# Fetching more single tiles of rows from SyncE and ScalarE in a graph network kernel, with byte offsets kept in the edge records

## What is computed

```python
h = relu(layernorm(x)); x = x + attention(h)      # q[src]·k[dst], softmax over the edges of each dst, sum of v[src]
h = relu(layernorm(x)); x = x + relation(h)       # mean per edge type of (h @ W[type])[other end], edges both ways
h = relu(layernorm(x)); x = x + gine(h)           # sum of h[dst] + attr16 @ We over the edges of each src, then an MLP
h = relu(layernorm(x)); x = x + edge_conv(h)      # relu(sum of (h @ W)[src] + attr6 @ We over the edges of each dst)
```

## Time and profile before

| | us |
|---|---|
| timed, median of 3 runs | 21892.74 |
| timed, lowest and highest | 21871.51, 21898.5 |
| profiled execution, first to last instruction (the span) | 15054.0 |
| median of the timed runs less that span | 6838.7 |

### The profile page before, as it was taken

The page is one execution under the profiler, slowest core; times in us unless marked ns, Lnnn a source line. Parts: engine busy times, 40 slices in busy tenths (PEclk is TensorE's granted clock), DMA queues, the critical chain, the costliest instruction groups (busy, mean ns, idle before and its releaser), DMA issues. The chain is left out here.

```text
span 15054.0 us, 271220 instructions
## 1 busy us (share of the span) xinstructions
PE 8740.4 (58%) x56159; PEld 6734.5 (45%) x56575; DVE 9778.7 (65%) x34050; ACT 2787.6 (19%) x7303; POOL 11087.4 (74%) x11347
## 2 busy tenths in 40 slices
PE   6766667777777777555555555555444444544444
PEld 2212226666666666244444444444333333433334
DVE  8877777777878778866666677777533333433334
ACT  0011114444444444421111111111100000200000
POOL 4777767777777777777777777777677777477776
PEclk8866668999999999865555555555555555655555
DMA  2011122222222222422222222222222222422222
GB/s 85 7 42 50 53 59 74 69 69 69 69 69 69 69 69 67 152 83 59 59 58 59 58 63 63 62 63 63 69 63 63 63 62 60 121 59 59 58 59 68
DMA packets 734382, 992.39 MB, mean 66 GB/s; under 512 B 271737, under 2 KB 534898, under 8 KB 732626
## 3 DMA queue, kind: packets, MB, share of 16 engines
q0 software_dynamic: 387968, 670.55, 17.1%
q1 hardware_dynamic: 324786, 301.13, 6.5%
q10 hardware_dynamic: 20000, 3.33, 0.1%
HBM read 795.25 MB, written 178.86 MB: 65 GB/s over the span
## 5 line engine op out<-in xcount | busy, mean ns | idle before, releaser
L1834 DVE TENSOR_TENSOR acc<-banks,acc 128x128 f32 x3328 | 969.8, 291 | 2616.2 <-PE banks L1792 2247.3
L668 POOL DMA_INDIRECT rec_dst<-stage_dst_sort,row_dst_sort x1563 | 1575.4, 1008 | 641.1 <-issue 474.3
L800 POOL DMA_INDIRECT far_att<-table_qv,recs_att x1664 | 1636.5, 983 | 523.9 <-issue 506.8
L800 POOL DMA_INDIRECT far_sum_dst<-table_h,recs_dst x1613 | 1561.2, 968 | 584.1 <-issue 491.7
L800 POOL DMA_INDIRECT far_sum_src<-table_h,recs_src x1613 | 1572.9, 975 | 558.8 <-issue 491.6
L800 POOL DMA_INDIRECT far_rel_src<-table_xw,recs_rel_src x1638 | 1574.7, 961 | 508.7 <-issue 494.2
L800 POOL DMA_INDIRECT far_rel_dst<-table_xw,recs_rel_dst x1638 | 1561.1, 953 | 510.4 <-issue 494.5
L1622 DVE TENSOR_TENSOR acc<-banks,acc 128x128 f32 x3328 | 969.7, 291 | 1119.2 <-PE banks L1548 1002.5
L936 POOL DMA_INDIRECT rec_src<-moved_att,row_src x1248 | 1245.0, 998 | 397.3 <-issue 379.9
L1792 PE MATMUL banks<-far_sum_src,hot_sum_src 128*128 128x128 f32 x3226 | 825.1, 436 | 1214.9 <-DVE hot_sum_src L1825 831.3
L1792 PE MATMUL banks<-far_sum_dst,hot_sum_dst 128*128 128x128 f32 x3226 | 825.9, 436 | 1147.5 <-DVE hot_sum_dst L1825 899.8
(11 more groups left out here) (343 smaller groups left out, 21302.0 us busy)
## 6 DMA issues: line engine op xcount, KB each, us to landing
lone_sync_rel_dst<-table_xw SPq DMA_DIRECT2D x3328, 0.5 KB
lone_sync_rel_src<-table_xw SPq DMA_DIRECT2D x3328, 0.5 KB
lone_sync_sum_src<-table_h SPq DMA_DIRECT2D x3328, 0.5 KB
lone_sync_sum_dst<-table_h SPq DMA_DIRECT2D x3328, 0.5 KB
lone_scalar_sum_src<-table_h ACTq DMA_DIRECT2D x3200, 0.5 KB
lone_scalar_sum_dst<-table_h ACTq DMA_DIRECT2D x3200, 0.5 KB
table_xw<-xw_rel_tables SPq DMA_DIRECT2D x98, 512.0 KB
far_att<-table_qv,recs_att POOLq DMA_INDIRECT x1664
```

What stands on the lines that cost most here:

```text
L668: e.indirect_dma_start(out=flat_dst, out_offset=bass.IndirectOffsetOnAxis(ap=row["dst"][:, c + i:c + i + 1], axis=0), in_=stage["dst"][:, ...
L800: e.indirect_dma_start(out=self.far[:, g % RING, t, :], out_offset=None, in_=table, in_offset=bass.IndirectOffsetOnAxis(ap=index, axis=0)) ...
L1834: e.tensor_tensor(acc[:, bass.ds(at[t], 1), :], sums[g0 % 4][:, t:t + 1, :], acc[:, bass.ds(at[t], 1), :], ALU.add).then_inc(k.s_sum, 1)
```

## The change

- Each record gets two more words, `OFF` and `OFF8`: where the far row begins in `table_h` and in `table_xw`, in bytes. The dst records get a third, `OFFQ`, for `table_qv`. ACT writes them in `staged`. The column of ones becomes `OFF`; records are 13 and 22 words instead of 11 and 21.
- `single_rows` replaces `number_rows` and `fetch_rows`: it loads 32 registers with one instruction (`LOAD`), and addresses the table as a flat array of bytes at the register's value.
- Single tiles come at a step of their own in each pass (`Lone(buffer, ids, column, tile, first, step)`): SP every 6th group in the attention (69 tiles, which was 0), every 10th in the relation and sum passes (41 tiles each, which was 26); ACT every 16th in the relation passes (25 tiles, which was 0), every 10th in the sum passes (41, which was 25).
- ACT issues its rows a few after each group, in the relation passes behind its copy of that group (L1538), in the sum passes in a loop over the groups.
- In the attention DVE's two operations on gathered rows are split in two in the groups with a single tile.

```diff
-IDX, IDX8, LOC, TYP, ONE, ATT = range(6)
-CD = ATT + 6
+IDX, IDX8, LOC, TYP, OFF, OFF8, ATT = range(7)
+ROW = F * 4
+LOAD = 32
+OFFQ = ATT + 6
+CD = OFFQ + 1
...
         def staged(e, s, j):
+            e.activation(to[:, b, 0:n, OFF].bitcast(I32), node[FAR[s]][:, c:c + n], ACT.Copy, scale=float(ROW))
+            e.activation(to[:, b, 0:n, OFF8].bitcast(I32), idx8[s][:, c:c + n], ACT.Copy, scale=float(ROW))
+            if s == "dst":
+                e.activation(to[:, b, 0:n, OFFQ].bitcast(I32), node[FAR[s]][:, c:c + n], ACT.Copy, scale=float(2 * ROW))
             e.wait_ge(s_att[s][b], 16 * (j // 2 + 1))
...
+class Lone:
+    def __init__(self, buffer, ids, column, tile, first, step):
+        self.buffer, self.ids, self.column, self.tile, self.step = buffer, ids, column, tile, step
+        self.groups = list(range(first, GROUPS, step))
...
-        for p in range(first, first + n, 8):
-            row = e.bass.values_load_multi_w_load_instructions(
-                self.ids[name][0:1, s % 2, p:p + 8], engines=[e.engine], min_val=0, max_val=table.shape[0] - 1,
-            for i in range(8):
-                e.dma_start(self.lone[name][p + i:p + i + 1, s % 2, :], table[bass.ds(row[i], 1), :]).then_inc(self.k.s_lone[name][s % 2], 16)
+    def single_rows(self, e, name, g, n, table, freed):
+        one = self.lone[name]
+        r, end = (min(P * h // one.step, P * len(one.groups)) for h in (g, g + n))
+        width = table.shape[1] * 4
+        flat = table.rearrange("n f -> (n f)").bitcast(U8)
+        while r < end:
+            s, first = divmod(r, P)
+            m = min(P - first, end - r)
+            if first == 0:
+                if s == 0:
+                    self.number_rows(e, name, 0)
+                if s >= 2:
+                    e.wait_ge(*freed(one.groups[s - 2]))
+                e.wait_ge(self.k.s_ids[name], self.ids_base[name] + 16 * (s + 1))
+                if s + 1 < len(one.groups):
+                    self.number_rows(e, name, s + 1)
+            for p in range(first, first + m):
+                if p % LOAD == 0:
+                    one.at = e.bass.values_load_multi_w_load_instructions(
+                        one.ids[0:1, s % 2, p:p + LOAD], engines=[e.engine], min_val=0, max_val=(table.shape[0] - 1) * width,
+                row = flat[bass.ds(one.at[p % LOAD], width)].rearrange("(a n) -> a n", a=1)
+                e.dma_start(one.buffer[p:p + 1, s % 2, :].bitcast(U8), row).then_inc(self.k.s_lone[name][s % 2], 16)
+            r += m
...
 def attention_pass(k):
+        lone = {"sync": Lone(sb("lone_sync", [P, 2, 2 * F]), sb("ids_sync", [1, 2, P], I32), OFFQ, GT - 1, 5, 6)}
...
                 e.dma_start(moved[:, b, :, :], k.raw_src[:, c * MOVE:(c + 1) * MOVE, :]).then_inc(k.s_moved[b], 16)
+                st.single_rows(e, "sync", c * RG, RG, k.table_qv, lambda g: (s_mix, g + 1))
...
-                    e.tensor_tensor(qk[:, :, :], st.far[:, g4 % RING, :, 0:F], key_rows, ALU.mult).then_inc(s_score, 1)
+                    n = len(st.tiles(g4))
+                    i = e.tensor_tensor(qk[:, 0:n, :], st.far[:, g4 % RING, 0:n, 0:F], key_rows[:, 0:n, :], ALU.mult)
+                    if n < GT:
+                        i = e.tensor_tensor(qk[:, n, :], st.far_rows(g4, n)[:, 0:F], key_rows[:, n, :], ALU.mult)
+                    i.then_inc(s_score, 1)
...
 def relation_pass(k, side):
+        lone = {"sync": Lone(spent[0].bitcast(F32), spent[2][0:1, :, :], OFF8, GT - 1, 9, 10),
+                "scalar": Lone(spent[1].bitcast(F32), spent[3][0:1, :, :], OFF8, GT - 2, 19, 16)}
+        freed = lambda g: (k.s_product, p0 + g + 1)
...
                 e.copy(hot_t[:, g % 4, :, :], turned[g % 2]).then_inc(k.s_flat, 1)
+                st.single_rows(e, "scalar", g, 1, k.table_xw, freed)
...
 def sum_pass(k, side):
+        lone = {"sync": Lone(sb("lone_sync", [P, 2, F]), old, OFF, GT - 1, 9, 10),
+                "scalar": Lone(sb("lone_scalar", [P, 2, F]), sb("ids_scalar", [1, 2, P], I32), OFF, GT - 2, 13, 10)}
```

More of the change, by code:

```diff
@@ L29 @@
 GROUPS = -(-TILES // BT) * RG
-LONE = 16
-LONES = GROUPS // LONE
-assert GROUPS % LONE == 0
 NT = GROUPS * GT
@@ L786, in fetcher @@
     def fetcher(self, g, t):
[L788 to L791, removed]
+        for name, one in self.lone.items():
+            if t == one.tile and g in one.groups:
+                return name
+        return None
     def tiles(self, g):
@@ L807, in far_rows @@
         name = self.fetcher(g, t)
-        return self.lone[name][:, g // LONE % 2, :] if name else self.far[:, g % RING, t, :]
+        if name is None:
+            return self.far[:, g % RING, t, :]
+        one = self.lone[name]
+        return one.buffer[:, one.groups.index(g) % 2, :]
     def fetched(self, e, g):
@@ L834, in fetch_rows @@
-    def fetch_rows(self, e, name, s, table, first, n):
-        for p in range(first, first + n, 8):
-            row = e.bass.values_load_multi_w_load_instructions(
-                self.ids[name][0:1, s % 2, p:p + 8], engines=[e.engine], min_val=0, max_val=table.shape[0] - 1,
-                skip_runtime_bounds_check_because="the sort writes numbers of rows of the table alone")[1]
-            for i in range(8):
-                e.dma_start(self.lone[name][p + i:p + i + 1, s % 2, :], table[bass.ds(row[i], 1), :]).then_inc(self.k.s_lone[name][s % 2], 16)
+                s = self.lone[name].groups.index(g)
@@ L849, in close @@
         self.k.rec_base += 16 * (BLOCKS // NREC)
-        if self.far is not None:
-            self.k.ring_base = [self.gathered(GROUPS - RING + r)[1] for r in range(RING)]
-        for name in self.lone:
+        self.k.ring_base = [self.gathered(GROUPS - RING + r)[1] for r in range(RING)]
+        for name, one in self.lone.items():
+            self.k.ids_base[name] += 16 * len(one.groups)
             for b in range(2):
-                self.k.lone_base[name][b] += 16 * P * self.turns(name, LONES - 2 + (LONES - 2 + b) % 2)
+                self.k.lone_base[name][b] += 16 * P * len(range(b, len(one.groups), 2))
 assert BLOCKS % NREC == 0 and GROUPS % RING == 0
@@ L874, in attention_pass @@
         top = sb("top", [P, W + 1, H])
-        st = Stream(k, "dst", sb("recs", [P, NREC, BT, CD]), sb("far", [P, RING, GT, 2 * F]))
+        lone = {"sync": Lone(sb("lone_sync", [P, 2, 2 * F]), sb("ids_sync", [1, 2, P], I32), OFFQ, GT - 1, 5, 6)}
+        st = Stream(k, "dst", sb("recs", [P, NREC, BT, CD]), sb("far", [P, RING, GT, 2 * F]), lone)
         win = k.win["dst"]
```

122 lines of the change are left out of this document (43 added, 79 removed).

## The result

The changed kernel takes 23993.65 us, median of 4 runs (23936.95 to 24004.96), and the kernel before, beside it, 21895.62 (21871.51 to 21903.32): ratio 1.0961, 95% interval 1.0947 to 1.0974. Forecast were 21730 us and a range up to 23000, so both sign and range were wrong. The profiled execution took 23988.55 us.

The account below looks back on a forecast made before the run. POOL, issuing one indirect DMA after another, was taken as the bound. The terms -268.7 + 100 + 5 gave -164 us in the span, so 21892.7 - 164 = 21729, called 21730 us; range 21600 to 23000.

Parts of the forecast that it names:

- the load of 32, T: SP's load of 32 registers for single rows: taken as 0.8 us, bounds 0.78 and 3.13.
- the 6839 us: Time outside the traced span, in no row of the profile: left as it is, no change.
- S = 45.3 + 4T: SP's time for one single tile: 48.5 us, against 53.3 available in the attention, 48.3 and 48.5 in the passes.
- The value of 1.15: Load time T in us from which SP as the bound would decide the result.
- SP becomes the bound: Rival: a load costs by the register, T = 3.13, so SP limits attention and passes; 23450 us, slower, chance 0.13.
- the one with the fixed part: Rival: SP's load has a fixed part and smaller slope, T = 1.3; 22000 us, slower, chance 0.10.
- The row: SP's step for each single row without the register operation: 0.339 us, bounds 0.27 and 0.417.
- The gathers removed: POOL's gathers saved in attention, relation and sum passes: 88.9, 100.7 and 79.1 us, together 268.7 us.
- Contention at POOL, +100: POOL's gathers lengthened by more single rows beside them: 200 us in all or nothing, half taken, 100 us.
- The sort, +5: ACT's additional small instructions in the sort: nothing to 22 us, 5 taken.
- The rival on the time outside the span: Rival: time outside the span grows with 33300 more instructions at 25 ns, 0.84 ms; slower, chance 0.03.
- The third rival: SP's register operation stays or a move replaces it: S = 57.5, 23440 us, slower, chance 0.06.

Follow-up runs that it names:

- e10: The kernel before, unchanged, run for its trace with nothing held up: 15005.29 us.
- e18: The changed kernel, unaltered, in a set where nothing is held up: 15699.55 us, ratio 1.0456 to the kernel before.
- e3: The changed kernel with 8 registers a load instead of 32, nothing held up: 16720.3 us.
- e5: The changed kernel, unaltered, timed in rounds, held up: 23970.93 us, ratio 1.0944 to the kernel before.
- e8: The changed kernel with the single tiles of the kernel before, held up: 20480.76 us, ratio 0.9361 to the kernel before.
- e14: The changed kernel with all single tiles gathered by POOL, held up: 19647.85 us, ratio 0.8839 to the kernel before.
- e9: The changed kernel with all single tiles gathered by POOL, nothing held up: 15190.2 us, ratio 1.0117 to the kernel before.
- e4: The changed kernel with the single tiles of the kernel before, nothing held up: 15081.9 us.
- step 11: The changed kernel with SP's passes and ACT's sum passes at every 11th group, not 10th; held up, 23217.02 us (1.0613) and 23463.26 us (1.0561).

## Why the prediction was wrong

First to last gather of POOL in us, nothing held up (before from e10, after from e18), and after held up:

| | before | after | after, held up |
|---|---|---|---|
| attention | 3762 | 3724 | 6124 |
| relation, dst and src | 2055, 2063 | 2183, 2184 | 3253, 3270 |
| sum, src and dst | 2052, 2051 | 2282, 2282 | 3412, 3387 |

Two terms failed. The forecast was 21730 and 23994 was measured, 2264 us more. The load of 32 accounts for 794 of them, by the prediction's own formula with the measured load in it, and the 6839 us that were left as they are for the other 1471.

- **The step that failed: the load of 32, T.** It was set to 0.8 us, "the nearest row is SP's own". T is 2.13. With 0.785 for 8 (e3), 24 more registers cost 1.34 us: 0.056 each on a fixed 0.34 (a line through two points). The rows on which it hung allowed this; the choice put them aside in favour of the lower bound. The Trainium skill ("DMA: Bandwidth & Descriptors", Latency and other measured facts) has a floor of about 600 ns for a register load. The loads of 4 at 0.33 and 0.34 us and the line's fixed part are below it, and the 1.3 worked out from it is short as well.
- **The form of the sum was right.** S = 45.3 + 4T with T = 2.13 is 53.8, measured 53.3 and 54.9. The value of 1.15 from which SP decides was passed by far. By the prediction's own formula four passes are 4 × (41 × 53.8 + 30) = 8943 us instead of 8242, the attention 69 × 53.8 = 3712 instead of 3788, the sort +5: +630 in all in place of -164, and +688 was measured where nothing is held up (e18). The rival "SP becomes the bound" had the mechanism, and the one with the fixed part had the shape; T lies between their 1.3 and 3.13.
- **The row.** No register operation, a move of 29 and a DMA of 228: right. 26 rows without a load take 8.33 us, a step of (8.33 - 0.23) / 25 = 0.324 against 0.339.
- **The gathers removed.** The counts came as predicted, the time didn't: the attention gives back 38 us of 88.9, since 69 tiles at 53.3 us are 3678, hardly below POOL's own. The other passes give back nothing: each is 122 to 231 us longer.
- **Contention at POOL, +100.** About right, but it doesn't stand out. A gather takes 955, 962, 981, 979 and 989 ns (relation dst and src, sum src and dst, attention) against 953, 961, 975, 968 and 983, 41 us over all of them; against the same kernel's 950, 955, 968, 967 and 973 in e10 it is 84 us, with 66 single tiles in a relation pass for 26 and 82 in a sum pass for 51.
- **The sort, +5.** Nothing held up, 2070 us against 2075.
- **ACT.** A load of 2.19 to 2.26 us makes its tile longer than thought, but PE waits for none of them.
- **The other step that failed: "the 6839 us outside the span".** They were inside, as the difference between two conditions of execution. The span and the timed runs could not belong together, and a trace of the timed condition was missing; I had a sum for a kernel of 15.05 ms. With T right, that sum gives 15054 + 630 + 6839 = 22523; 1471 us of the 23994 stay, and they are what the hold-up adds to this change: it shows in SP's tile, 88 us in the attention and 82 in the last sum pass for 53 and 55. The rival on the time outside the span named a growth with instructions, 0.84 ms, but as a fixed price in another place.
- **Two slips in the sums.** The third rival's 23440 doesn't follow from its S of 57.5: the formula gives 23380. The value of T at which the sign turns is 1.14, not 1.15. Neither changes the range or the forecast.

Held up, the change goes in three parts (e5 to e8): byte offsets and big loads -1404 us, the attention's tiles +795, the passes' +2695. SP is late throughout: already with the old tiles, where the first part ends, it goes through the last sum pass without a pause (e8). The price of a row isn't fixed. It is 22 ns for a row that nobody reads, 69 on the average over the old tiles, 245 in the last 24 tiles of the passes.

**Open.** What holds the engines up isn't settled. What was seen: a set of runs, and so a chip, has it for all its kernels; SP and ACT show pauses of 0.6 to 0.8 us, POOL doesn't. It doesn't need single rows: without any (e14) the sort takes 3272 us for 2078 (e9) and the attention 5384 for 3764. The mean granted TensorE clock is lower in it, 0.607 against 0.686 (after and e18), but PE is then busy 9481 us for 8583 and DVE 9732 for 9720, so longer instructions don't fill the 8.3 ms between them. Traces taken in it hold fewer semaphore records (102335 for 284373 in e8 and e4, the same program), so a pause without a releaser may have one. That each recorded event costs was only argued, and no trace shows the kernel before held up. Whether step 11 or the attention's tiles alone win anything where nothing is held up wasn't measured: their runs met the other condition.

**Which version to take.** Old tiles with byte offsets and loads of 32: 15081.9 us beside 15067.55, and ratio 0.9361 held up. Without any single tiles: 1.0117 and 0.8839. Where nothing is held up no run beat the kernel before.

## What to carry to other kernels

Moving work off the engine that is the bound pays only as long as the helper keeps its own period, and a helper that also issues the bound engine's inputs (here SP's record loads) passes its lateness on at once. When one unseen duration decides on which side of the period the helper falls, say at what value the sign turns (here 1.14 us, between bounds of 0.78 and 3.13), and don't take the cheap bound without a row for it. When the timed median and the traced span differ by a third, no forecast of the time stands before one knows which condition each belongs to.

## What the runs showed of the hardware

- A register load from SBUF on SP: 0.78 us for 8, 2.07 to 2.13 for 32; on ACT 0.83 and 2.25 to 2.26 (sum passes). Big loads save a third, not three quarters.
- A value that is already in bytes takes a register operation of 37 ns and its gap out of each DMA of a row: 0.324 us a row, 0.417 before.
- The same program took 15.70 ms in one set of runs and 23.97 to 24.26 in others, the kernel before 15.01 to 15.07 and 21.88 to 22.25. How much a kernel loses by the hold-up differs: 19.6 ms without single tiles, from 15.2.
- Held up, an engine that issues many small instructions becomes late where it had slack: with the old tiles a tile took SP 105.2 us for the 79 of POOL's gathers beside it, where otherwise SP waited 652 us in that pass.
